# An attention block on one core: x's transposing transfers go one to a body, into waiting places that VectorE copies home, and VectorE writes the projection's bias

## The chip, the cores and the metric

The kernel runs on one core of one Trainium2 chip. The metric is the device time of one execution in microseconds (us). The engines are TensorE (PE; its weight loads are listed as PEld), VectorE (DVE), ScalarE (ACT), GpSimd (POOL) and SyncE (SP), which here issues transfers only. A row with a q behind the engine (SPq, ACTq) belongs to that engine's sequencer.

## What is computed

The reference, cut to what matters (16 batches of 1024 rows of 512 values, 8 heads of 64):

```python
qkv = (x @ w_qkv).reshape(b, n, 3, H, hd).transpose(2, 0, 3, 1, 4)
q, k, v = (qkv[0], qkv[1], qkv[2])
attn = jnp.einsum('bhnd,bhmd->bhnm', q, k) * scale
attn = jnp.where(attn_mask[None, None] == 0, -jnp.inf, attn)
attn = jax.nn.softmax(attn, axis=-1)
o = jnp.einsum('bhnm,bhmd->bhnd', attn, v).transpose(0, 2, 1, 3).reshape(b, n, d)
o = o @ w_proj + b_proj
ln = (o - mu) * jax.lax.rsqrt(var + LN_EPS) * ln_gamma + ln_beta
x = _layernorm(x + (o + ln), axis=-1)
```

## The kernel before

**Bodies.** The work is cut into 64 groups g: one batch (g // 4) and one pair of heads (g % 4). Each engine's program is a row of bodies, one for each group, with one before them and some behind for the last projections. Bodies 5 to 62 are a loop that the engines run from one piece of code; the others stand written out one after another. A body has 8 units (128 query rows each) of 4 slots, and what each engine does in which slot is fixed by tables (`ORDER`, `TAKE_ACT`, `TAKE_DVE`, `NORM_SLOTS`, `XT_UNIT`).

**A head's path.** In a unit, TensorE writes the scores of the two heads of the pair (L401). VectorE adds the mask and takes the row's minimum of the negated scores (L638). ScalarE takes the exponential (L494) and, one unit later, its float16 high part (L507). GpSimd subtracts it for the low part (L742). SyncE then issues one transposing transfer of both parts, `pt<-p_split` (L307, `turn`). `p_split` has 4 places, so that ScalarE's high part of a head waits until the transfer of the head four before it has landed. Three units after the scores TensorE multiplies by V (L422 to L424). There are 16 such transfers in a body. I call a head by its unit and half: (4,b) is the second head of unit 4.

**Side work.** Between these TensorE does the next group's Q and K (`Q0`, `K0`, `K1`, `Q1`; L360), V (`V0`, `V1`; L347), the transposes of the output (`O0`, `O1`; L342) and, four bodies late, the projection of two row tiles (`P0`, `P1`; L383). The first part of the projection's list has 12 matmuls a tile, and a 13th one adds the bias: a matrix of ones times two bias rows (L386). ScalarE and VectorE take each result from one of two PSUM banks as a high and a low part; the next user of the bank waits for that. `O0`, the last transposes of a body, waits for VectorE's low part of K0 (`k_lo`, L627), and that for ScalarE's `k_hi` (L487).

**x.** TensorE needs x transposed (`xt`). Each body loads two tiles of the next batch into `x_in` (L541, ScalarE's queue, slot 1), ScalarE and GpSimd split them into `x_split` (L465, L776), one place for each body of a batch. In the last body of each batch (g % 4 == 3) SyncE issues all four transposing transfers `xt<-x_split` (L285, `turn_x`), two ahead of unit 2's heads and two ahead of unit 3's; in the loop each pair stands under `If((g & 3) == 3)` blocks (L238). `Q0`, which starts in slot 16, waits for the first two, `K1` for the others. The first batch's x goes through the same transfers before the bodies.

**The projection's row tile** is then normalised on VectorE (L667 to L697, in pieces), with the residual and layer norm; `summed` tells that its bank is free.

Of the kernel before, what the change touches and what calls it, by code (L numbers as in the profile page):

```python
# [9 lines left out]
P = 128  # L10
# [18 lines left out]
BIAS_LO = 32  # L29
# [4 lines left out]
ORDER = [("Q1", 0, 12), ("V0", 0, 48), ("V1", 0, 48), ("P0", 0, 4), ("O1", 0, 4), ("P0", 4, 13), ("Q0", 0, 12),  # L34
         ("K0", 0, 12), ("K1", 0, 12), ("P1", 0, 9), ("O0", 0, 4), ("P1", 9, 13)]
# [3 lines left out]
LENGTH = {"Q1": 12, "V0": 48, "V1": 48, "O1": 4, "Q0": 12, "K0": 12, "K1": 12, "O0": 4, "P0": 13, "P1": 13}  # L39
COST = {"Q": 9, "V": 2.5, "O": 5, "K": 9, "P": 9}  # L40
FIRST_GROUP, LAST_GROUP = -1, GROUPS + PAIRS
LOOP = (PAIRS + 1, GROUPS - 1)


def items_by_slot():
# [4 lines left out]
    for kind, i in items:  # L50
# [12 lines left out]
XT_UNIT = [3, 3, 4, 4]  # L63
NORM_SLOTS = [{"stats": 19, "aggr": 20, "eps": 20, "add": 20, "power": 21, "scale": 23, "sum": 24, "stats2": 27,
               "aggr2": 28, "eps2": 28, "power2": 29, "shift": 29, "out": 30},
              {"stats": 30, "aggr": 33, "eps": 33, "add": 34, "power": 35, "scale": 34, "sum": 38, "stats2": 38,
# [72 lines left out]
def attention_block(nc, x, adj, w_qkv, w_proj, b_proj, gamma, beta, out):  # L139
# [3 lines left out]
    with ExitStack() as ctx:  # L143
# [17 lines left out]
        x_split = sb("x_split", [P, T // 2, 2, 2, D], F16)  # L161
        xt = sb("xt", [P, T, 2, KC, P], F16)
# [23 lines left out]
        ones = sb("ones", [P, P], F16)  # L186
        bias_rows = sb("bias_rows", [P, D], F16)
# [8 lines left out]
        x_first = p32[:, :, :].rearrange("p t (two d) -> p t two d", two=2)  # L196
# [12 lines left out]
        bias_ready, bias_zero = sem("bias_ready"), sem("bias_zero")  # L209
        w_hi_ready, w_ready, mask_ready = sem("w_hi_ready"), sem("w_ready"), sem("mask_ready")  # L210
        x_first_loaded, x_in_loaded = sems("x_first_loaded", T // 2), sem("x_in_loaded")
        x_hi_done, x_lo_done, x_turned = sem("x_hi_done"), sem("x_lo_done"), sems("x_turned", 2)
# [22 lines left out]
        def transposing(eng, g, do):  # L235

            if not known(g):
                with eng.If((g & 3) == 3):  # L238
                    do()
            elif (g + 1) % PAIRS == 0 and 0 <= batch(g + 1) < B:  # L240
                do()

# [29 lines left out]
        def _(sp):  # L272
            for t in range(T // 2):
                sp.dma_start(x_first[:, t, :, :], x_pairs[t, :, :, :]).then_inc(x_first_loaded[t], 16)
# [4 lines left out]

            def turn_x(g, p):  # L280

                wait_alone(sp, x_lo_done, batch(g + 1) * (T // 2) + (p + 1))
                if not known(g) or g >= 0:
                    wait_alone(sp, side_ready, side_done(g, "V1"))
                sp.dma_start_transpose(xt[:, 2 * p:2 * p + 2, :, :, :].rearrange("p t h k n -> p (t h k) n"),  # L285
                                       x_split[:, p, :, :, :].rearrange("p t h d -> p (t h d)")
                                       ).then_inc(x_turned[p // 2], 16)

            for p in range(T // 2):
                turn_x(FIRST_GROUP, p)  # L290
# [19 lines left out]

            def body(g):
                for u in range(UNITS):
                    for p in range(T // 2):
                        if u == XT_UNIT[p] and not (known(g) and g == FIRST_GROUP):
                            transposing(sp, g, lambda: turn_x(g, p))
# [10 lines left out]
        def _(pe):  # L326
            pe.wait_ge(ident_ready, 1)

            def side_matmul(g, kind, i):
# [13 lines left out]
                elif kind[0] == "V":  # L343
# [3 lines left out]
                    mm = nc.tensor.matmul(bank[:, c * P:(c + 1) * P], xt[:, t, rows, k, :], w[:, k, OF_V, pair(g), :],  # L347
                                          start=(i == 0), stop=(i % 12 == 11), skip_group_check=True)
                else:
                    k, part = i // 3, i % 3  # L350
                    if part == 0 and known(g) and g < 0 and kind == NEXT_FIRST:
                        pe.wait_ge(w_ready, 2 * (k + 1))
                    if i == 0 and kind == NEXT_FIRST:
                        wait_alone(pe, x_turned[0], batch(g + 1) * 32 + 32)
                    if i == 0 and kind == "K1":
                        wait_alone(pe, x_turned[1], batch(g + 1) * 32 + 32)
                    w, x_half = (w_hi, w_hi, w_lo)[part], (HI, LO, HI)[part]
                    p = pair(g if kind == "Q1" else g + 1)
# [7 lines left out]
            def project(g, half, i):  # L366
                c, t = batch(g - PAIRS), pair(g) * 2 + half
                if i == 0:
                    if known(g) and g == PAIRS and half == 0:
                        pe.wait_ge(w_ready, 4 * KC)  # L370
                        pe.wait_ge(bias_ready, 4)
                    if known(g) and g >= GROUPS:
                        pe.wait_ge(min_done, heads(GROUPS, 0, 0))
                        pe.wait_ge(summed, projected(g, half) - (1 if g > GROUPS or half else 0))
                    else:
                        wait_alone(pe, summed, projected(g, half))
# [4 lines left out]
                if i < 3 * KC:  # L381
                    k, part = i // 3, i % 3
                    mm = nc.tensor.matmul(proj_bank(g, half), ot[:, (HI, LO, HI)[part], parity(c), k, t, :],  # L383
                                          (wp_hi, wp_hi, wp_lo)[part][:, k, :], start=(i == 0), stop=False)
                else:
                    nc.tensor.matmul(proj_bank(g, half), ones[:, :], bias_rows[:, :], start=False, stop=True).then_inc(proj_ready, 1)  # L386
# [39 lines left out]

            def body(g):
# [12 lines left out]
        def _(act):  # L440
# [5 lines left out]
            def prepare_projection():  # L446
                act.wait_ge(wp_loaded, 16 * KC)
                for kc in range(KC):
                    nc.scalar.activation(wp_hi[:, kc, :], wp_in[:, kc, :], ACT.Copy, scale=WSCALE).then_inc(w_hi_ready, 1)
                act.wait_ge(const_loaded, 64)  # L450
                act.wait_ge(bias_zero, 1)
                nc.scalar.activation(bias_rows[0:1, :], x_res[0:1, 0, :], ACT.Copy, scale=WSCALE).then_inc(bias_ready, 1)
                nc.scalar.activation(p_split[BIAS_LO:BIAS_LO + 1, 0, LO, 0:D], x_res[BIAS_LO:BIAS_LO + 1, 0, :], ACT.Copy,
                                     scale=WSCALE).then_inc(bias_ready, 1)

            def first_split(p):
                act.wait_ge(x_first_loaded[p], 16)
                nc.scalar.activation(x_split[:, p, :, HI, :], x_first[:, p, :, :], ACT.Copy).then_inc(x_hi_done, 1)

            def split(g):  # L460
                if known(g) and not 0 <= batch(g) < B - 1:
                    return
                wait_alone(act, x_turned[1], batch(g) * 32 + 32)
                wait_alone(act, x_in_loaded, g * 16 + 16)
# [360 lines left out]
```

## Time and profile before

| | |
|---|---|
| median of 3 runs | 3231.33 us (3230.16 to 3237.03) |
| the profiled execution | 3231.68 us |
| its span in the trace | 3229.8 us |
| PE busy | 2994.3 us (93%) |
| POOL busy | 2628.1 us (81%) |
| ACT busy | 2624.1 us (81%) |
| DVE busy | 2197.0 us (68%) |
| granted TensorE clock | 0.973 |

Busy times are sums over the span. A matmul's end is modelled, so that a busy PE says that it had work, not that it was at its peak. The granted clock is the share of 2.4 GHz that TensorE was given; 0.50 is the lower level, 1.2 GHz.

### The profile page before, as it was taken

What the parts mean: (1) busy time and instruction counts of PE and PEld (TensorE: products, weight loads), DVE (VectorE), ACT (ScalarE), POOL (GpSimd) and SP (SyncE); (2) the same over time, 40 slices, a digit from 0 to 9 for tenths busy, and PEclk for the clock granted to TensorE, in tenths of its full rate; (3) what the DMA queues carried; (4) which work ended last, traced back from release to release, by engine and by line L of the source; (5) the groups of instructions that cost most, each with busy time, mean ns of one, the idle gap of its engine ahead of it and who ended that gap; (6) DMA issues with size and microseconds to landing.
All of it is one profiled execution on the core that took longest, in us unless ns stands there. A gap on an engine that the chain in (4) does not pass through costs nothing.

```text
span 3229.8 us, 119607 instructions
## 1 busy us (share of the span) xinstructions
PE 2994.3 (93%) x42112; PEld 1842.0 (57%) x42112; DVE 2197.0 (68%) x4243; ACT 2624.1 (81%) x3790; POOL 2628.1 (81%) x1610
## 2 busy tenths in 40 slices
PE   5889999899998999999999998999999899999995
PEld 2556556565565556656566565556556566565562
DVE  4546667677676767767677676767767677676775
ACT  5878878788787878878788787888888788787882
POOL 4768878788787878878798797888878788787884
PEclk9989999999999999999999999999999999999997
DMA  8999999999999999999999999999999999999994
GB/s 225 192 199 195 211 214 218 218 208 220 211 212 218 215 214 219 216 212 219 214 216 214 215 213 222 216 215 220 216 214 219 212 212 219 212 215 218 216 208 108
DMA packets 2320778, 682.49 MB, mean 211 GB/s; under 512 B 2268498, under 2 KB 2268498, under 8 KB 2320724
## 3 DMA queue, kind: packets, MB, share of 16 engines
q1 hardware_dynamic: 2266724, 581.58, 97.3%
q10 hardware_dynamic: 54000, 100.16, 9.7%
q8 instruction: 37, 0.61, 0.1%
q14 instruction: 17, 0.14, 0.0%
HBM read 77.60 MB, written 33.55 MB: 34 GB/s over the span
## 4 chain that ended last, share of the span: by engine, by line
POOL 54%; issue 29%; SPq 7%; PE 6%; DMA 2%; DVE 1%; POOLq 1%; ACT 1%; ACTq 0%; DVEq 0%
POOL p_split L742 42%; SPq L307 5%; POOL x_res L758 4%; POOL x_split L776 4%; POOL norm L766 2%; POOL norm L761 2%; PE scores_a L401 1%; PE side L360 1%; SPq L285 1%; DMA pt<-p_split 1%; PE side L347 1%; POOL shift L769 1%; POOLq L741 1%; PE proj L383 0%; PE pv_bank L422 0%
## 5 line engine op out<-in xcount | busy, mean ns | idle before, releaser
L742 POOL TENSOR_TENSOR p_split<-p,p_split 128x1024 f16<-128x1024 f32 x1024 | 2172.4, 2138 | 531.8 <-ACT p_split L507 526.0
L494 ACT ACTIVATE p<-p,row_min 128x1024 f32<-128x1024 f32 x1024 | 1167.9, 1142 | 91.9 <-DVE row_min L638 89.8
L507 ACT ACTIVATE p_split<-p 128x1024 f16<-128x1024 f32 x1024 | 1053.6, 1046 | 206.8 <-DMA pt<-p_split 205.9
L638 DVE CUSTOM_DVE_ANT_0 p<-scores_a,mask_q 128x1024 f32<-128x1024 f32 x512 | 626.9, 1224 | 502.3 <-PE scores_b L401 481.9
L422 PE MATMUL pv_bank<-v_both,pt 128*128 128x64 f16 x8192 | 840.0, 195 | 26.5 <-DMA pt<-p_split 24.6
L424 PE MATMUL pv_bank<-v_both,pt 128*128 128x64 f16 x8192 | 840.6, 195 | 0.0
L423 PE MATMUL pv_bank<-v_both,pt 128*128 128x64 f16 x8192 | 840.5, 195 | 0.0
L422 PEld LDWEIGHTS pv_bank<-v_both,pt 128*128 128x128 f16 x8192 | 747.9, 99 | 115.2 <-issue 39.6
L360 PE MATMUL side<-xt,w_hi 128*128 128x512 f16 x2048 | 683.2, 391 | 119.3 <-DMA xt<-x_split 114.3
L423 PEld LDWEIGHTS pv_bank<-v_both,pt 128*128 128x128 f16 x8192 | 736.9, 99 | 84.4 <-issue 6.0
L424 PEld LDWEIGHTS pv_bank<-v_both,pt 128*128 128x128 f16 x8192 | 737.4, 99 | 0.0
L638 DVE CUSTOM_DVE_ANT_0 p<-scores_b,mask_q 128x1024 f32<-128x1024 f32 x512 | 624.6, 1220 | 6.6 <-POOL p_split L742 0.5
L347 PE MATMUL side<-w_hi,xt 128*128 (+1 forms) x4096 | 399.0, 219 | 1.5 <-DVE q_lo L627 1.5
L360 PE MATMUL side<-xt,w_lo 128*128 128x512 f16 x1024 | 397.9, 389 | 0.0
L360 PEld LDWEIGHTS side<-xt,w_hi 128*128 (+1 forms) x2048 | 187.5, 99 | 349.8 <-issue 221.2
L347 PE MATMUL side<-w_lo,xt 128*128 (+1 forms) x2048 | 367.0, 220 | 0.0
L347 PEld LDWEIGHTS side<-w_hi,xt 128*128 128x128 f16 x4096 | 317.0, 98 | 36.6 <-issue 29.1
L383 PE MATMUL proj<-wp_hi,ot 128*128 128x512 f16 x992 | 329.4, 384 | 2.6 <-issue 2.6
L401 PE MATMUL scores_a<-k_hi,q_hi 64*128 64x512 f16 x1024 | 311.4, 385 | 6.1 <-DVE row_min L638 4.5
L401 PE MATMUL scores_b<-k_hi,q_hi 64*128 64x512 f16 x1024 | 311.6, 385 | 0.0
L401 PE MATMUL scores_b<-k_lo,q_hi 64*128 64x512 f16 x1024 | 304.3, 377 | 0.0
L401 PE MATMUL scores_a<-k_lo,q_hi 64*128 64x512 f16 x1024 | 304.2, 377 | 0.0
(80 smaller groups left out, 4261.3 us busy)
## 6 DMA issues: line engine op xcount, KB each, us to landing
x_in<-in_x ACTq DMA_DIRECT2D x63, 512.0 KB, 5.1
x_res<-in_x ACTq DMA_DIRECT2D x120, 256.0 KB, 3.3
out<-x_res ACTq DMA_DIRECT2D x120, 256.0 KB, 3.7
pt<-p_split SPq DMA_TRANSPOSE x1024, 4.8
pt<-in_adj SPq DMA_DIRECT2D x8, 512.0 KB, 9.7
ot<-in_L_gnn_w_qkv SPq DMA_DIRECT2D x4, 768.0 KB, 9.8
p<-in_x SPq DMA_DIRECT2D x4, 512.0 KB, 5.3
p<-in_x ACTq DMA_DIRECT2D x8, 256.0 KB, 8.5
```

Of the source, the lines that this page charges most:

```text
L307: sp.dma_start_transpose(pt[:, head % TURNED, :, :, :].rearrange("p h t n -> p (h t) n"), p_split[:, head % RING, :, :].rearrange("p h n - ...
L347: mm = nc.tensor.matmul(bank[:, c * P:(c + 1) * P], xt[:, t, rows, k, :], w[:, k, OF_V, pair(g), :], start=(i == 0), stop=(i % 12 == 11), ...
L360: mm = nc.tensor.matmul(bank[:, :].rearrange("p (t n) -> p t n", t=4), w[:, k, what, p, :], xt[:, 4 * half:4 * half + 4, x_half, k, :], st ...
L383: mm = nc.tensor.matmul(proj_bank(g, half), ot[:, (HI, LO, HI)[part], parity(c), k, t, :], (wp_hi, wp_hi, wp_lo)[part][:, k, :], start=(i ...
L401: mm = nc.tensor.matmul(scores[ab][:, keys], left[rows, q], right[rows, keys], start=(n == 0), stop=(n == 2))
L422: nc.tensor.matmul(o, hi, v_hi, start=(kt == 0 and at == 0), stop=False, skip_group_check=True)
L423: nc.tensor.matmul(o, hi, v_lo, start=False, stop=False, skip_group_check=True)
L424: mm = nc.tensor.matmul(o, lo, v_hi, start=False, stop=(kt == T - 1), skip_group_check=True)
L494: nc.scalar.activation(p32[:, slot, :], p32[:, slot, :], ACT.Exp, bias=row_min[:, slot:slot + 1], scale=-1.0, accum_out=row_sum[:, head:he ...
L507: nc.scalar.activation(p_split[:, head % RING, HI, :], p32[:, head % RING, :], ACT.Copy).then_inc(hi_done, 1)
L638: nc.vector.tensor_tensor_reduce(out=p32[:, slot, :], in0=scores[ab][:, :], in1=mask_q[:, u, :], scale=-SCALE, scalar=3.0e38, op0=ALU.add, ...
L742: nc.gpsimd.tensor_tensor(p_split[:, slot, LO, :], p32[:, slot, :], p_split[:, slot, HI, :], ALU.subtract).then_inc(lo_done, 1)
```

## The change

x's transfers: in every body SyncE issues one `turn_x`, ahead of unit 3's heads, without an `If`. It goes to a waiting place at the end of `xt` (the fourth pair of tiles goes straight home). In a batch's last body VectorE copies the six waiting tiles home, one in each of the slots 12 to 17, and `Q0` waits for the last copy (`x_copied`). `K1` of every body waits for that body's transfer. `x_split` has one place instead of four, and x is loaded in slot 12 instead of slot 1. The first batch's x is transposed by TensorE instead, with ScalarE and VectorE splitting it.

The bias: VectorE writes it into the projection's bank (`seed`) after the bank's last reader, and the 12 matmuls add to it; the 13th is gone. The loop ends at body 58 instead of 62, so that bodies 59 to 62 are now written out.

```diff
-ORDER = [... ("P0", 4, 13), ... ("P1", 9, 13)]
+ORDER = [... ("P0", 4, 12), ... ("P1", 9, 12)]
-LOOP = (PAIRS + 1, GROUPS - 1)
+LOOP = (PAIRS + 1, GROUPS - PAIRS - 1)
-XT_UNIT = [3, 3, 4, 4]
+XT_UNIT = 4
+LOAD_X = 12
+COPY = [12, 13, 14, 15, 16, 17]
-               {"stats": 30, "aggr": 33, ...
+               {"stats": 30, "aggr": 31, ...
-        x_split = sb("x_split", [P, T // 2, 2, 2, D], F16)
-        xt = sb("xt", [P, T, 2, KC, P], F16)
+        x_split = sb("x_split", [P, 2, 2, D], F16)
+        xt = sb("xt", [P, T + 6, 2, KC, P], F16)
+        def place(t):
+            return t - 4 if t >= 4 else t + 10
+        def waiting(g):
+            return 8 - pair(g) * 2
+            def turn_x(g):
+                wait_alone(sp, x_lo_done, g + 1)
+                wait_alone(sp, side_ready, side_done(g, "V1"))
+                wait_alone(sp, x_copied, batch(g))
+                sp.dma_start_transpose(xt[:, bass.ds(waiting(g), 2), :, :, :]...
-                    for p in range(T // 2):
-                        if u == XT_UNIT[p] and not (known(g) and g == FIRST_GROUP):
-                            transposing(sp, g, lambda: turn_x(g, p))
+                    if u == XT_UNIT and active(g, "X"):
+                        turn_x(g)
+                    if i == 0 and kind == "K1" and active(g, "X"):
+                        wait_alone(pe, x_turned, g * 16 + 16)
                     if i == 0 and kind == NEXT_FIRST:
-                        wait_alone(pe, x_turned[0], batch(g + 1) * 32 + 32)
-                    if i == 0 and kind == "K1":
-                        wait_alone(pe, x_turned[1], batch(g + 1) * 32 + 32)
+                        wait_alone(pe, x_copied, batch(g + 1))
-                    nc.tensor.matmul(proj_bank(g, half), ones[:, :], bias_rows[:, :], start=False, stop=True).then_inc(proj_ready, 1)
+            def copy_tile(g, t):
+                if t == 0:
+                    wait_alone(dve, side_ready, side_done(g, "V1"))
+                    wait_alone(dve, x_turned, g * 16)
+                move = nc.vector.tensor_copy(xt[:, place(t), :, :, :]..., xt[:, 8 - t // 2 * 2 + t % 2, :, :, :]...)
+            def seed(g, i):
+                nc.vector.tensor_scalar(proj_bank(g, i), bias_b[:, :], WSCALE, None, ALU.mult).then_inc(seeds(g, i)[0], 1)
-                    if s == 1:
+                    if s == LOAD_X:
                         load_next(g)
```

SyncE's program in the loop, around the transfers of units 2 and 3. Before, from the second head of unit 1 to the first head of unit 2 (L307 is a head's transfer, L285 one of x, L238 the `If`, L135 a wait):

```order
L307 DMA_TRANSPOSE pt<-p_split 128x16x128
L238 REGISTER_ALU
L238 COMPARE_AND_BRANCH
L135 ISA x2
L285 DMA_TRANSPOSE xt<-x_split 128x16x128
L238 UNCONDITIONAL_BRANCH
L238 COMPARE_AND_BRANCH
L135 ISA x2
L285 DMA_TRANSPOSE xt<-x_split 128x16x128
L238 UNCONDITIONAL_BRANCH
L135 REGISTER_ALU x2
L307 DMA_TRANSPOSE pt<-p_split 128x16x128
```

The same engine now, from the second head of unit 2 to the first head of unit 3 (L310 is a head's transfer, L319 that of x):

```order
L310 DMA_TRANSPOSE pt<-p_split 128x16x128
L137 REGISTER_ALU
L137 ISA
L137 REGISTER_ALU
L319 REGISTER_ALU x2
L319 ISA
L319 DMA_TRANSPOSE xt<-x_split 128x16x128
L137 REGISTER_ALU x2
L310 DMA_TRANSPOSE pt<-p_split 128x16x128
```

The branches are gone, and the x transfer, which stood under them, now runs in every body between two heads' transfers.

VectorE's program in the loop from the low part of V1 on (slot 12), where unit 3's two masked minima stand. Before:

```order
L621 SCALAR_TENSOR_TENSOR v_both<-side,v_both 128x8x64
L135 REGISTER_ALU
L638 ISA p,row_min<-scores_a,mask_q 128x1024
L638 ISA row_min 128x1
L135 REGISTER_ALU
L638 ISA p,row_min<-scores_b,mask_q 128x1024
```

and now (L655 is a copy, L242 its `If`, L668 the masked minimum):

```order
L641 SCALAR_TENSOR_TENSOR v_both<-side,v_both 128x8x64
L242 REGISTER_ALU
L242 COMPARE_AND_BRANCH
L655 COPY xt<-xt 128x1024
L242 UNCONDITIONAL_BRANCH
L137 REGISTER_ALU
L668 ISA p,row_min<-scores_a,mask_q 128x1024
L668 ISA row_min 128x1
L242 COMPARE_AND_BRANCH
L655 COPY xt<-xt 128x1024
```

A copy under an `If` now stands between each two of VectorE's steps here; the sixth one stands behind unit 4's first masked minimum.

## Rows read from the trace of the kernel before

**Rows 1.** The page, its first line.

```profile
span 3229.8 us, 119607 instructions
```

**Rows 2.** Windows: a body with one batch's heads only, and a batch's last body.

```profile
core 0: us, PE busy (x) PEld busy (x) DVE busy (x) ACT busy (x) POOL busy (x), PEclk, DMA share, GB/s
1120.90:1167.20 46.30, 45.79 (x659) 28.33 (x658) 34.05 (x66) 40.86 (x60) 40.87 (x26) 1.00 1.08 214
1167.20:1222.90 55.70, 48.07 (x661) 29.29 (x661) 34.05 (x66) 40.75 (x60) 40.99 (x26) 0.94 1.10 217
```

**Rows 3.** Waits: waiter, releaser, us in total, times, longest us.

```profile
ACT p_split L507 <- DMA pt<-p_split: 205.9, 216, 3.3
...
PE side L360 <- DMA xt<-x_split: 114.3, 16, 26.1
```

**Rows 4.** Timeline of SP: issues of head (7,a), three bodies (start us, us).

```profile
1125.56 3.07 SPq L307 DMA_TRANSPOSE pt<-p_split  x1
...
1171.84 3.56 SPq L307 DMA_TRANSPOSE pt<-p_split  x1
...
1227.49 3.42 SPq L307 DMA_TRANSPOSE pt<-p_split  x1
```

**Rows 5.** Timeline of ACT: high part of head (6,b), the same two bodies.

```profile
1162.59 1.06 ACT L507 ACTIVATE p_split<-p 128x1024 f16<-128x1024 f32 x1 [1.13 <-DMA pt<-p_split]
...
1218.25 1.06 ACT L507 ACTIVATE p_split<-p 128x1024 f16<-128x1024 f32 x1 [1.16 <-DMA pt<-p_split]
```

**Rows 6.** Timeline of SP: issues around the two places with `If` blocks.

```profile
1140.52 2.38 SPq L307 DMA_TRANSPOSE pt<-p_split  x1
...
1143.62 1.95 SPq L307 DMA_TRANSPOSE pt<-p_split  x1
...
1145.86 3.77 SPq L307 DMA_TRANSPOSE pt<-p_split  x1
...
1150.30 1.92 SPq L307 DMA_TRANSPOSE pt<-p_split  x1
```

**Rows 7.** Line L307, single transfers issued at 1119.5, 1121.9 and 1125.6.

```profile
DMA to landing us min/median/max: 4.5/4.5/4.5
...
DMA to landing us min/median/max: 6.1/6.1/6.1
...
DMA to landing us min/median/max: 6.2/6.2/6.2
```

**Rows 8.** Groups by line: shapes xcount | busy us, mean ns | idle before.

```profile
L742 POOL TENSOR_TENSOR p_split<-p,p_split 128x1024 f16<-128x1024 f32 x1024 | 2172.4, 2138 | 531.8 <-ACT p_split L507 526.0
...
L386 PE MATMUL proj<-bias_rows,ones 128*128 128x512 f16 x124 | 48.8, 393 | 0.0
...
L594 DVE TENSOR_SCALAR mask_q<-pt 128x1024 bf16<-128x1024 f32 x8 | 5.3, 686 | 11.8 <-DMA pt<-in_adj 11.8
```

**Rows 9.** Timelines of DVE and PE around Q0 in a batch's last body.

```profile
1191.72 1.23 DVE L638 CUSTOM_DVE_ANT_0 p<-scores_a,mask_q 128x1024 f32<-128x1024 f32 x1 [1.19 <-PE scores_b L401]
...
1197.43 0.61 PE L360 MATMUL side<-xt,w_hi 128*128 128x512 f16 x1 [5.69 <-DMA xt<-x_split]
```

**Rows 10.** Windows: the stretch of low clock behind that wait.

```profile
1195.00:1201.80 6.80, 4.37 (x32) 2.45 (x33) 0.00 (x0) 0.62 (x2) 1.69 (x1) 0.50 1.06 196
```

**Rows 11.** Windows: batches 2 and 14, the first and last of 13; body 4; bodies 60 to 62.

```profile
442.60:637.30 194.70, 185.90 (x2635) 114.56 (x2636) 136.63 (x265) 164.13 (x238) 164.45 (x101) 0.98 1.09 217
...
2778.60:2972.90 194.30, 185.80 (x2635) 114.37 (x2636) 135.40 (x263) 162.25 (x235) 163.19 (x100) 0.98 1.08 214
2972.90:3111.00 138.10, 137.24 (x1975) 84.91 (x1974) 101.95 (x198) 121.87 (x178) 122.34 (x76) 1.00 1.09 217
...
239.60:287.80 48.20, 47.11 (x661) 28.52 (x658) 30.28 (x58) 39.93 (x59) 39.24 (x22) 0.97 1.16 195
```

**Rows 12.** Timeline at the start: PE waits for the low part of Q0.

```profile
38.87 1.01 PE L360 MATMUL side<-xt,w_hi 128*128 128x512 f16 x2 [5.02 <-DVE q_lo L627]
```

**Rows 13.** Timeline of DVE in the last projections.

```profile
3203.53 0.75 DVE L686 SCALAR_TENSOR_TENSOR p<-scores_a,norm,p 128x512 f32<-128x512 f32 x1 [1.51 <-POOL norm L761]
```

More of the change, by code:

```diff
@@ L233, in bodies, with at_end @@
                 body(g)
[L235 removed]
+        def at_end(eng, g, do):
             if not known(g):
@@ L257, in proj_bank, with seeds @@
             return scores[0][:, 0:CH] if known(g) and g >= GROUPS and i == 1 else proj[:, :]
+        def seeds(g, i):
+            if known(g) and g >= GROUPS:
+                return (seeded[0], projected(GROUPS, 0) + (g - GROUPS + 1)) if i == 0 else (seeded[1], g - GROUPS + 1)
+            return seeded[0], projected(g, i) + 1
         def last_tile(g, i):
@@ L327, in _, with first_turn @@
             pe.wait_ge(ident_ready, 1)
+            def first_turn(t):
+                pe.wait_ge(x_first_loaded[t], 16)
+                wait(pe, x_first_lo, t - 1)
+                for k in range(KC):
+                    mm = nc.tensor.transpose(side[t % 2][:, k * P:(k + 1) * P], x_first[:, t, k * P:(k + 1) * P], ident[:, :])
+                mm.then_inc(x_first_turned, 1)
             def side_matmul(g, kind, i):
@@ L370, in project @@
                         pe.wait_ge(w_ready, 4 * KC)
[L371 to L376, printed above, removed]
+                    wait_alone(pe, *seeds(g, half))
                     if half == 0:
@@ L425, in times_v @@
                 mm.then_inc(pv_done, 1)
+            for t in range(T):
+                first_turn(t)
+            for k in range(KC):
+                mm = nc.tensor.matmul(proj[:, k * P:(k + 1) * P], ident[:, :], ident[:, :], start=(k == 0), stop=True,
+                                      skip_group_check=True)
+            mm.then_inc(bits_set, 1)
             def body(g):
@@ L449, in prepare_projection, with first_high @@
                     nc.scalar.activation(wp_hi[:, kc, :], wp_in[:, kc, :], ACT.Copy, scale=WSCALE).then_inc(w_hi_ready, 1)
[L450 to L464, printed above, removed]
-                nc.scalar.activation(x_split[:, pair(g), :, HI, :], x_in[:, :, :], ACT.Copy).then_inc(x_hi_done, 1)
+            def first_high(t):
+                act.wait_ge(x_first_turned, t + 1)
+                nc.scalar.activation(xt[:, place(t), HI, :, :], side[t % 2][:, :].rearrange("p (k n) -> p k n", k=KC), ACT.Copy
+                                     ).then_inc(x_first_hi, 1)
             def take(g, kind):
```

150 lines of the change are left out of this document (81 added, 69 removed).

## The prediction

> **What bounds the kernel now.** I read the body's length first. A body takes 46.3 us, and a batch's last body 55.7 [rows 2]; 13 batches in a row take 2530.3 us, 194.6 each [rows 11]. So a batch's last body costs 9.4 us more than the others, and the obvious reason is the wait that the change goes for: TensorE waits 114.3 us in 16 pieces for x's transfers [rows 3], 5.7 us of it in the body shown [rows 9], and behind it the clock is at its lower level (0.50, 1.2 GHz) for 6.8 us [rows 10], which loses 3.4. Together 9.1 of the 9.4 us. In the other bodies TensorE has work for 45.8 of 46.3 us [rows 2], which looks like a kernel that TensorE bounds.
>
> Then I followed the other engines round a body, because ScalarE also waits for transfers, 205.9 us in 216 pieces [rows 3]. SyncE's queue issues head (7,a) at 1125.56, 1171.84 and 1227.49 [rows 4]: laps of 46.28 and 55.65 us, the bodies' own lengths. Each lap has two legs. On the first, SyncE issues twelve heads with next to nothing between them, until (4,b) lands; that lets ScalarE write the high part of (6,b), which the trace shows as a wait ended by a transfer, at 1162.59 and at 1218.25 [rows 5]. On the second leg come ScalarE's steps up to the high part of (7,a), GpSimd's low part and the next issue of (7,a). The second leg is 9.25 us in the one body and 9.24 in the other. The first is 37.03 and 46.41 us. **So the lap is made of the transfer leg and a fixed rest, in both kinds of body,** and the last body's 9.38 us are four x transfers in the queue's leg. TensorE's wait is a second road to nearly the same length, and taking it away alone gives nothing back. This is the step on which all else rests.
>
> **An x transfer in every body.** It is issued between (2,b) and (3,a), within the first leg. Four of them lengthen it by 9.38 us [rows 4, 5], 2.35 each. But the body without x transfers pays for the `If` blocks: SyncE stands still for 0.72 us (1142.90 to 1143.62) and 0.67 us (1149.63 to 1150.30), where 0.29 is usual (1145.57 to 1145.86) [rows 6], 0.8 us too much, and the change drops them. If such gaps cost their full length, an x transfer is (9.38 + 0.8) / 4 = 2.55 us and the change adds 2.55 - 0.8 = 1.75 a body; if they cost nothing it adds 2.35. I take 1.7, since the queue has no idle time in this leg into which a gap could fall.
>
> **The load of x_in** moves from slot 1 to slot 12. Now it lies across the start of the leg: a head's transfer takes 4.5 us to land before it, and 6.1 (outside the leg) and 6.2 us (its first) beside it [rows 7]. In slot 12 all it delays is inside. If the second delay is only the first one handed on, moving costs nothing; if they are two, 1.6 us. I take 0.5, nearer the lower end, as 6.2 also holds a store of the same time.
>
> A body is then 46.3 + 1.7 + 0.5 = **48.5 us**, with bounds 46.3 + 1.7 = 48.0 and 46.3 + 2.35 + 1.6 = 50.3. Below that I keep 47.4 as a rival.
>
> **What TensorE saves.** Two bias matmuls a body, at most 0.39 us each [rows 8], so TensorE needs about 45.4 of the 48.5 us. This is worth nothing: it makes TensorE's wait at `O0` longer, which is where a late lap shows. `K1` waits in each body for its own x transfer; that lands about when K1 starts, and a wait there comes out of the 3 us at `O0`.
>
> **VectorE's seeds** are two more steps a body of at most 0.69 us (L594, twice their elements [rows 8]), beside 34 us of work in 46 [rows 2]: hidden in the bodies. In the last projections VectorE idles only 1.51 us at a time for GpSimd [rows 13], once in two tiles, so of 1.4 us a pair of tiles some 0.9 shows, four times: +3.5.
>
> **The copies** are six in a batch's last body. The trace has no copy between float16 tiles; the nearest row is L594, 1024 elements from SBUF to SBUF in 0.69 us [rows 8], and I take that, between 0.3 and the 1.23 us of the masked minimum [rows 9]. The sixth copy stands behind unit 4's first masked minimum, which starts at 1191.72, about when TensorE is ready for Q0 (1197.43 - 5.69 = 1191.74) [rows 9]. So Q0 cannot start before 1191.7 + 1.2 + 0.7 + 0.2 for the semaphore: TensorE waits 2.1 us, and 2.6 if copies two to five make VectorE half a microsecond late. If the clock then halves for half as long as in rows 10, this costs another 1.7. TensorE's road through the last body is 45.4 + 0.3 + 2.6 + 1.7 = 50.0, longer than the lap; with 0.3 for what is left of an earlier low clock, 50.3 us.
>
> **The sum.** A batch: 3 x 48.5 + 50.3 = 195.8 against 194.6, +1.2, and 13 of them +15.6. Batches 0 and 1 hold eight x transfers before and after: +1. Bodies 60 to 62 take 46.0 us each; they leave the loop, and straight-line body 4, which has no x transfer either, takes 48.2 [rows 11]: +6.5. At the start TensorE waits 5.0 us for Q0's low part [rows 12], which stands behind mask tiles whose loads SyncE issues after the x transfers; without these some 3 us go. Last projections +3.5. Together 15.6 + 1 + 6.5 - 3 + 3.5 = +23.6: a span of 3253.4 [rows 1], and with the 1.9 us outside it (3231.68 - 3229.8) 3255.3. The profiled execution is 0.35 us above the median of the runs. **Forecast: 3255 us**, with 3234 to 3285 as its own range (48.1 to 49.1 a body).
>
> **The rivals.**
>
> *The transfer leg grows less (chance 0.20).* If the gaps cost more than their length, or the moved load falls into time that the dropped `If` opens, a body is 47.4 and the last 49.3: 191.5 a batch, -40 in 13, and +5 outside: 3196 us. For it: the laps scatter, and the leg of 37.03 us holds other loads and stores. Against: nothing in rows 4 and 5 shows a transfer cheaper than 2.35.
>
> *TensorE is the bound after all (0.08).* Then a body is 45.7, the last 48.1 (2.4 of wait), 185.2 a batch, -122 in 13 and +1 outside: 3111 us. For it: 45.8 of 46.3 us busy. Against: the second leg's 9.24 and 9.25 us.
>
> *The copies stand still for GpSimd (0.22).* This is one mechanism on the other side of no change, and it decides from about 1 us per copy on. GpSimd's low part runs 2.14 us [rows 8], one after another. If a copy cannot run beside it, each of the last four or five waits for the rest of one; by hand the sixth ends at about 1199, so that TensorE waits 7.5 us, more than now, with a longer low clock: 45.4 + 0.3 + 7.5 + 2.8 = 56.0 for the last body, 5.7 more than above in 15 batches, +85: 3340 us. The trace cannot speak for or against it: VectorE's wide steps there read PSUM, and L594 ran while GpSimd had no work. The Trainium skill speaks for it: "SBUF — State Buffer", section "Who interferes with whom", says that VectorE and GpSimd share a port pair under an exclusive lock, held for a whole instruction, when VectorE runs in a two-port mode; and "VectorE: DVE Perf Modes", section "The perf-mode tier table", puts a 16-bit copy within SBUF into such a mode, at four elements a cycle. By the second page alone a copy would take an estimated 0.4 us (1024 elements at four a cycle and the fixed cost that it gives) and the last body would be some 0.3 us shorter; by both pages, the 3340 stands. No run shows either yet.
>
> *The low clock comes in every body (0.06).* A wait of about 3 us at `O0` may halve the clock each time; it decides once TensorE's road passes the lap, 48.5 - 45.4 = 3.1 us, that is if 3 us of wait and more than 0.1 of lost clock add up. With 50 us a body and 51.8 the last: 201.8 a batch, 3333 us.
>
> *The time is only moved (0.06).* The four transfers cost the same wherever they stand, and all else cancels: 3232 us.
>
> **From these to the numbers.** The forecast has 0.38. A measurement of this kernel can tell about 0.2%, 6.5 us, from no change. Faster by more: 0.19 of the first rival, the second's 0.08: 0.27. Within it: 0.06, 0.01 of the first and 0.04 of the forecast's lower edge: 0.11. Slower: the rest of the forecast 0.34, 0.22 and 0.06: 0.62. The range 3185 to 3335 leaves out the second rival, about half of the third and some of the fourth, under 2 in 10.
>
> **What would show it.** SyncE's laps: 48 to 49 us between issues of (7,a) in every body, the second leg still 9.2 us, TensorE's wait at `O0` grown from under 1 us to 2 or 3. A copy's duration, and when the sixth ends against the masked minimum before it: right behind it, and the last body is about 50 us; 5 us later, and it is the lock. The prediction is wrong if the second leg shrinks when the first grows, for then the lap was not what it seemed; or if bodies come down to 45.6.

## The result and the profile after

The changed kernel takes 3360.73 us (median of 4 runs, 3353.94 to 3365.36), the kernel before in runs beside it 3232.34: the ratio is 1.0394, with a 95% interval of 1.0371 to 1.0416. It is slower, as forecast, but by 128 us instead of 24, and it lies 26 us above the range.

The page's first line, to [rows 1]:

```profile
span 3363.5 us, 119057 instructions
```

The span grew by 133.7 us. I cut it at the bodies' starts as before [rows 11]. Windows of a batch's four bodies (24 to 27), of the two stretches of low clock in them, of bodies 8 to 11 (batch 2), of bodies 60 to 62 and of all behind them; columns as in [rows 2]:

```profile
1259.70:1308.40 48.70, 45.76 (x657) 27.93 (x656) 35.22 (x68) 40.97 (x60) 41.51 (x27) 1.00 1.04 210
1308.40:1358.00 49.60, 46.40 (x657) 28.07 (x656) 35.61 (x69) 41.66 (x61) 41.64 (x26) 0.98 1.07 214
1358.00:1407.80 49.80, 46.63 (x657) 28.14 (x656) 34.81 (x68) 40.23 (x59) 40.41 (x26) 0.98 1.05 208
1407.80:1461.30 53.50, 47.12 (x657) 29.02 (x656) 42.45 (x74) 41.39 (x60) 41.09 (x25) 0.94 1.00 201
1356.40:1359.80 3.40, 3.40 (x24) 1.17 (x22) 1.96 (x5) 3.29 (x6) 1.83 (x2) 0.51 1.15 212
1434.90:1441.80 6.90, 3.39 (x30) 2.02 (x31) 4.89 (x7) 2.48 (x4) 2.85 (x2) 0.51 0.97 189
447.70:650.00 202.30, 186.19 (x2595) 112.30 (x2595) 146.74 (x276) 163.07 (x234) 162.88 (x101) 0.97 1.03 205
3085.90:3232.00 146.10, 138.36 (x1971) 84.66 (x1972) 105.63 (x205) 118.73 (x176) 117.36 (x74) 0.99 1.14 196
3232.00:3363.50 131.50, 78.72 (x865) 44.97 (x864) 76.94 (x160) 49.59 (x70) 65.85 (x62) 0.79 0.69 125
```

A plain body is 48.7 to 49.8 us, where I had 48.5, and the last one 53.5, where I had 50.3. The 13 batches of [rows 11] went from 194.6 to 202.9 us each: 108 of the 133.7 us. The rest lies in the bodies behind them (257.0 us before, 277.6 now) and before them (5.1).

SyncE's issues of (7,a), to [rows 4] (timeline of SP, four laps):

```profile
1264.74 2.29 SPq L310 DMA_TRANSPOSE pt<-p_split  x1
...
1313.42 2.42 SPq L310 DMA_TRANSPOSE pt<-p_split  x1
...
1362.29 1.89 SPq L310 DMA_TRANSPOSE pt<-p_split  x1
...
1412.82 2.32 SPq L310 DMA_TRANSPOSE pt<-p_split  x1
...
1466.32 2.31 SPq L310 DMA_TRANSPOSE pt<-p_split  x1
```

Laps of 48.7, 48.9, 50.5 and 53.5 us. TensorE's side of it, to [rows 3] (waits: waiter, releaser, us in total, times, longest):

```profile
ACT p_split L519 <- DMA pt<-p_split: 318.3, 251, 3.2
...
PE side L359 <- DVE k_lo L647: 129.6, 49, 3.8
...
PE side L380 <- DVE xt L655: 79.8, 15, 5.5
...
PE side L380 <- DMA xt<-x_split: 22.8, 37, 2.1
```

The wait for x's transfers (114.3 us) became one for the copies at `Q0`, 5.3 us in the mean of the last bodies (5.5 in the loop), and one of 2.6 us at `O0` in every plain body. In bodies 8 to 57 low clock follows the first in all 12 last bodies, the second in 18 of 38 plain ones. Now VectorE and GpSimd in that last body (timelines; L655 is a copy, L668 the masked minimum, L786 GpSimd's low part, L802 its bias):

```profile
1426.42 0.42 DVE L655 COPY xt<-xt 128x1024 f16<-128x1024 f16 x1
1426.75 1.22 DVE L668 CUSTOM_DVE_ANT_0 p<-scores_a,mask_q 128x1024 f32<-128x1024 f32 x1
...
1427.89 1.93 DVE L655 COPY xt<-xt 128x1024 f16<-128x1024 f16 x1
...
1431.49 4.28 DVE L655 COPY xt<-xt 128x1024 f16<-128x1024 f16 x3
1435.69 1.21 DVE L668 CUSTOM_DVE_ANT_0 p<-scores_a,mask_q 128x1024 f32<-128x1024 f32 x1
...
1436.83 1.20 DVE L655 COPY xt<-xt 128x1024 f16<-128x1024 f16 x1
```

```profile
1427.41 4.41 POOL L786 TENSOR_TENSOR p_split<-p,p_split 128x1024 f16<-128x1024 f32 x2
1431.77 1.45 POOL L802 TENSOR_TENSOR x_res<-x_res,beta_b 128x512 f32<-128x512 f32 x1
1433.27 4.49 POOL L786 TENSOR_TENSOR p_split<-p,p_split 128x1024 f16<-128x1024 f32 x2
```

What it does to the transfers (timeline of SP, heads (3,a), (3,b) and (4,a); the masked minimum of (4,a) is the one at 1435.69, behind three copies):

```profile
1439.48 4.94 SPq L310 DMA_TRANSPOSE pt<-p_split  x2
...
1448.26 1.91 SPq L310 DMA_TRANSPOSE pt<-p_split  x1
```

SyncE is done with the first two at 1444.42 and issues the third at 1448.26: 3.8 us idle inside the transfer leg, where 0.3 is usual there in a plain body. A smaller gap stands in every body, ahead of x's own transfer (L319), from 1436.67 to 1437.41, 0.7 us, where 0.3 is usual:

```profile
1424.54 12.13 SPq L310 DMA_TRANSPOSE pt<-p_split  x4
1437.41 1.78 SPq L319 DMA_TRANSPOSE xt<-x_split  x1
```

Line L655, all 90 copies (duration in ns: min/median/max):

```profile
L655 DVE COPY xt<-xt x90: 414/1204/2343, 209.3 to 3061.7; 128x1024 f16<-128x1024 f16 x90
```

One and the same copy takes 0.41 us, as the first one does, beside a GpSimd step of 128x1 only, or anything up to 2.34. The second begins at 1427.89, inside GpSimd's pair of low parts that began at 1427.41, and ends at 1429.82; the first of the two low parts ends at 1429.54, 0.3 us before it. GpSimd pays too: two low parts take 4.49 us where [rows 8] gives 2 x 2.14, and the bias 1.45 us.

### The profile page after: what moved, and what is told of

It reads as the page before. It is cut to its first block, busy times and chain, and to the rows that moved or that the text cites. A ratio compares the mean times of both kernels' runs of the same rounds, so it can differ in the third digit from the quotient of the medians.

```text
span 3363.5 us, 119057 instructions
## 1 busy us (share of the span) xinstructions
PE 3016.6 (90%) x42024; PEld 1833.9 (55%) x42024; DVE 2382.6 (71%) x4466; ACT 2635.4 (78%) x3789; POOL 2626.5 (78%) x1603
## 4 chain that ended last, share of the span: by engine, by line
POOL 34%; issue 22%; PE 20%; SPq 12%; DMA 5%; DVE 4%; ACT 1%; POOLq 1%; DVEq 0%; ACTq 0%
POOL p_split L786 27%; SPq L310 11%; PE scores_a L416 5%; DMA pt<-p_split 4%; PE side L364 4%; PE side L380 4%; POOL x_res L802 3%; POOL x_split L820 2%; PE proj L397 2%; PE pv_bank L437 2%; PE pv_bank L439 2%; PE pv_bank L438 2%; POOL norm L810 1%; SPq L319 1%; DVE xt L655 1%
## 5 line engine op out<-in xcount | busy, mean ns | idle before, releaser
L786 POOL TENSOR_TENSOR p_split<-p,p_split 128x1024 f16<-128x1024 f32 x1024 | 2180.2, 2144 | 661.4 <-ACT p_split L519 654.3
L668 DVE CUSTOM_DVE_ANT_0 p<-scores_a,mask_q 128x1024 f32<-128x1024 f32 x512 | 626.3, 1223 | 413.5 <-PE scores_b L416 323.6
L668 DVE CUSTOM_DVE_ANT_0 p<-scores_b,mask_q 128x1024 f32<-128x1024 f32 x512 | 623.9, 1219 | 3.4 <-POOL p_split L786 0.6
L397 PE MATMUL proj<-wp_hi,ot 128*128 128x512 f16 x992 | 315.8, 391 | 4.4 <-DVE proj L625 4.4
L416 PE MATMUL scores_b<-k_lo,q_hi 64*128 64x512 f16 x1024 | 311.1, 385 | 0.0
L416 PE MATMUL scores_a<-k_lo,q_hi 64*128 64x512 f16 x1024 | 311.1, 385 | 0.0
```

Of the source, the lines that this page charges most:

```text
L416: mm = nc.tensor.matmul(scores[ab][:, keys], left[rows, q], right[rows, keys], start=(n == 0), stop=(n == 2))
L668: nc.vector.tensor_tensor_reduce(out=p32[:, slot, :], in0=scores[ab][:, :], in1=mask_q[:, u, :], scale=-SCALE, scalar=3.0e38, op0=ALU.add, ...
L786: nc.gpsimd.tensor_tensor(p_split[:, slot, LO, :], p32[:, slot, :], p_split[:, slot, HI, :], ALU.subtract).then_inc(lo_done, 1)
```

## The experiments

All start from the changed kernel. Times stand against the kernel before, run beside each of them. The table gives mean body lengths in bodies 8 to 57 by place in the batch, worked out from the times at which unit 0's scores start in each trace, and the mean of 13 batches (bodies 8 to 59). e1, e4 and e11 leave something out and e12 adds a part of the projection twice: they price a term and are no kernels to use. The code is cut to the lines that matter.

| kernel | 1st | 2nd | 3rd | last | batch | median | ratio to before (95%) |
|---|---|---|---|---|---|---|---|
| before | 46.2 | 46.2 | 46.2 | 56.0 | 194.6 | 3232.3 | |
| after | 49.3 | 49.9 | 49.8 | 54.0 | 202.9 | 3360.7 | 1.0394 (1.0371 to 1.0416) |
| e1 small copies | 49.7 | 49.6 | 49.5 | 51.1 | 199.8 | 3313.1 | 1.0244 (1.0222 to 1.0266) |
| e2 reduce copies | 49.2 | 49.5 | 49.6 | 53.6 | 201.9 | 3349.4 | 1.0357 (1.0328 to 1.0386) |
| e3 load early | 48.6 | 48.7 | 49.2 | 53.9 | 200.3 | 3324.5 | 1.0280 (1.0259 to 1.0301) |
| e4 no seed | 49.2 | 49.9 | 49.7 | 54.1 | 203.0 | 3360.1 | 1.0386 (1.0353 to 1.0418) |
| e5 between bodies | 46.2 | 48.5 | 49.5 | 55.8 | 199.8 | 3318.8 | 1.0266 (1.0249 to 1.0283) |
| e6 pair copies | 50.0 | 49.5 | 49.6 | 49.8 | 198.9 | 3299.1 | 1.0200 (1.0180 to 1.0220) |
| e7 all three | 45.7 | 48.0 | 48.1 | 51.6 | 193.7 | 3231.2 | 0.9996 (0.9987 to 1.0006) |
| e8 idle Ifs | 49.5 | 50.1 | 50.3 | 54.8 | 204.8 | 3381.4 | 1.0459 (1.0441 to 1.0476) |
| e9 copies later | 45.6 | 48.1 | 48.0 | 50.2 | 192.3 | 3211.7 | 0.9935 (0.9916 to 0.9954) |
| e10 load in 20 | 47.3 | 49.5 | 48.7 | 51.2 | 196.6 | 3271.5 | 1.0120 (1.0100 to 1.0140) |
| e11 tiny x | 47.7 | 47.8 | 46.7 | 54.0 | 196.2 | 3271.5 | 1.0122 (1.0100 to 1.0145) |
| e12 more matmuls | 49.2 | 49.0 | 48.7 | 54.6 | 201.6 | 3343.5 | 1.0340 (1.0320 to 1.0359) |

**e1, the copies' time.**

```diff
-move = nc.vector.tensor_copy(xt[:, place(t), :, :, :]..., xt[:, 8 - t // 2 * 2 + t % 2, :, :, :]...)
+move = nc.vector.tensor_copy(xt[:, place(t), 0, 0, 0:2], xt[:, 8 - t // 2 * 2 + t % 2, 0, 0, 0:2])
```

> The six copies of a batch's last body move 2 elements instead of 1024 (x's tiles don't come home, so that Q, K and V of later batches are made of old x). Theory A (the copies, stretched by GpSimd's low parts, hold up the heads behind them, and the transfer queue runs dry in unit 4): a batch's last body falls from about 53.9 us to that of the others, 49.7, the second leg from 10.7 to 9.45, TensorE's wait at Q0 from 5.5 to under 0.5 us: 15 x 4.1 = 62 us less, 3300 us. Theory B (the copies' time lies beside the transfer leg and only TensorE's wait at Q0 moves elsewhere): under 10 us less, above 3350.

48 us less, nearer to A. The last body falls to 51.1 us, not to 49.7, and TensorE still waits 2.9 us at `Q0` (waits of e1). But this run does not take the copies' time away: line L655 and the second copy of a batch with GpSimd's pair of low parts beside it (timelines of e1):

```profile
PE side L380 <- DVE xt L655: 42.9, 15, 2.9
...
L655 DVE COPY xt<-xt x90: 156/441/2021, 205.1 to 3015.5; 128x2 f16<-128x2 f16 x90
...
1212.25 1.94 DVE L655 COPY xt<-xt 128x2 f16<-128x2 f16 x1
...
1212.03 4.23 POOL L785 TENSOR_TENSOR p_split<-p,p_split 128x1024 f16<-128x1024 f32 x2 [0.15 <-ACT p_split L519]
```

A copy of 2 elements takes 0.16 us or up to 2.02. The one shown begins inside a low part and ends with it (at 1214.19; half of the pair's 4.23 us is over at 1214.15), and the six of a batch still take 5.2 us of VectorE's time, against 8.0. So most of a copy's time is standing still and has nothing to do with its length. The shorter copies, which no longer stretch GpSimd's steps either, are worth 2.4 us of the wait and 2.9 us of the body; what the place of the sixth copy alone costs, behind unit 4's first masked minimum, this run doesn't show.

**e2, another form of the same copy.**

```diff
-move = nc.vector.tensor_copy(out, in_)
+move = nc.vector.tensor_reduce(out, in_.rearrange("... (n o) -> ... n o", o=1), axis=X, op=ALU.max)
```

> The copy is written as a tensor_reduce over an axis of one element, which moves the same 1024 elements. Theory A (the copy alone takes GpSimd's port and stands still for its step; this form does not): all six take one and the same time, about 1.1 us by the masked minimum's 1.22, whether GpSimd works beside them or not, GpSimd's steps beside them stay at 2.14 us instead of 2.3; the six sum to 6.7 us instead of 8.0 and the sixth ends 1.3 us earlier: 15 x 1.3 = 20 us less, 3341 us. Theory B (the stretching comes from GpSimd's own reads of SBUF and meets every form of VectorE's step): steps of up to 1.1 + 2.1 = 3.2 us, the sum above 9 us, 3375 us or more.

Line L655 and GpSimd's steps around 1432 in the trace of e2:

```profile
L655 DVE TENSOR_REDUCE xt<-xt x90: 1207/1211/1219, 209.4 to 3050.2; 128x1024 f16<-128x1024 f16 x90
```

```profile
1430.34 1.28 POOL L803 TENSOR_TENSOR x_res<-x_res,beta_b 128x512 f32<-128x512 f32 x1
1432.09 4.21 POOL L787 TENSOR_TENSOR p_split<-p,p_split 128x1024 f16<-128x1024 f32 x2 [0.46 <-ACT p_split L519]
```

All 90 take 1.21 us, beside GpSimd's steps or not, and these keep their 2.14 and 1.28 us. Same data, same places, same neighbours: the stretching belongs to the form of the copy. The median is 11 us lower though a lone copy takes three times as long; the intervals of the two ratios overlap, so that gain is at the edge of the noise, and it is the durations that rule out B. The six sum to 7.3 us here, against 8.0. What six copies of 0.42 us would cost unhindered, no run shows.

**e3, the load of x_in back in slot 1.**

```diff
-LOAD_X = 12
+LOAD_X = 1
-    wait_alone(act, x_lo_done, g + 1)
-    act.dma_start(x_in[:, :, :], x_pairs[g + (PAIRS + 1), :, :, :])
+    wait_alone(act, x_lo_done, g)
+    act.dma_start(x_in[:, :, :], x_pairs[g + PAIRS, :, :, :])
```

> x_in's load back in slot 1 (of the body that splits it), all else as after. Theory A (my term: in slot 12 the load lies inside the transfer leg and costs 0.5 us a body or more): 60 x 0.5 = 30 us less, 3331 us; the leg from the issue of (7,a) to the landing of (4,b) falls from 39.2 to about 38.7 us. Theory B (its place does not matter, as it delays one head's transfer wherever it stands): within 7 us of 3361. Theory C (the load is what makes x's transfer late for K1 and the clock fall at O0, so that it costs about 1.3 us in two bodies of four more): 3290 us.

36 us less, 0.6 a body, where I had 0.5: A. In the plain bodies it is 0.7, 1.1 and 0.6 us, 0.8 on average, and next to nothing in the last one, where SyncE's gap ahead of (4,a) grows from 4.2 us on average to 5.6 and takes it up. Low clock follows the wait at `O0` about as often as before (17 of 38 plain bodies), so that C is not what happens. `K1`'s wait for its x transfer falls from 22.8 to 4.7 us with it.

**e4, the seeds.**

```diff
-nc.vector.tensor_scalar(proj_bank(g, i), bias_b[:, :], WSCALE, None, ALU.mult)
+nc.vector.tensor_scalar(proj_bank(g, i)[:, 0:2], bias_b[:, 0:2], WSCALE, None, ALU.mult)
-    start=False
+    start=(i == 0)
```

> VectorE writes 2 of the bias's 512 columns (the bias is left out of the others) and TensorE's first matmul overwrites the bank: the seed keeps its place and its signals, its time falls from 0.70 to about 0.15 us. Theory A (hidden behind the laps in the bodies, seen only in the last projections): 3 us less, 3358 us. Theory B (VectorE's added work in units 1 and 6 delays the masked minimum behind it, and through ScalarE and GpSimd the transfer queue): 0.3 us or more a body, 3340 us or less.

No difference in the medians (0.6 us): the seeds are hidden.

**e5, x's transfers between the bodies.** `turn_x` no longer waits for V1 there, since the waiting place is free.

```diff
-if u == XT_UNIT and active(g, "X"): turn_x(g)
+if u == 0: with sp.If((g & 3) != 0): turn_x(g - 1)
-if u == XT_UNIT: turn_x(g)
+if u == XT_UNIT: with sp.If((g & 3) == 3): turn_x(g, True)
-wait_alone(pe, x_turned, g * 16 + 16)
+wait_alone(pe, x_turned, batch(g + 1) * 64)
```

> The x transfers of a batch's first three pairs go one body later, ahead of the issue of (7,a), where SyncE stands idle 1.1 to 2.5 us in the trace of after; only the fourth pair's stays in unit 4 of the last body. Theory A (a body's length is the transfer leg from the issue of (7,a) to the landing of (4,b), and x's transfer costs what it adds to that leg): the leg of the first three bodies falls by 2.0 to 2.4 us, from 39.6 to about 37.4, the second leg grows by 0.5 to 1.0 us, so a plain body is 1.5 us shorter and the last body no longer than now: 13 x 4.5 = 60 us less, 3300 us. Theory B (the DMA queues are the bound wherever the transfer stands in the lap): the body keeps its length, within 7 us of 3361.

42 us less, two thirds of A. By the definition of [rows 4, 5] the first leg of the three bodies fell from 40.1 to 36.8 us, by more than A has it, but the second grew from 9.5 to 11.9, not by 0.5 to 1.0. The timeline of SP shows why (L320 is the x transfer):

```profile
1346.07 2.15 SPq L320 DMA_TRANSPOSE xt<-x_split  x1
1348.55 3.34 SPq L310 DMA_TRANSPOSE pt<-p_split  x1
```

It is issued with (7,a) right behind it, so that it fills little of the idle time and pushes (7,a) back. The second leg is fixed only as long as nothing is put into it. The edit also brings two `If` blocks into each body of the loop, in e7, e9 and e10 too; e8 prices four of them at some 0.4 us a body.

**e6, three copies of two tiles, two of them behind V0.**

```diff
-COPY = [12, 13, 14, 15, 16, 17]
+COPY = [10, 11, 15]
+if t != 1: wait_alone(dve, side_ready, side_done(g, "V0" if t == 0 else "V1"))
+move = nc.vector.tensor_copy(xt[:, (10, 12, 0)[t]:(12, 14, 2)[t], :, :, :]..., xt[:, 8 - 2 * t:10 - 2 * t, :, :, :]...)
+if t == 1: move.then_inc(x_near, 1)      # Q0 waits for this one, K1 for x_copied
```

> Three copies of two tiles instead of six of one, in slots 10, 11 (behind V0 alone, for the tiles that Q0 and K0 read) and 15 (for K1), so that GpSimd's step can hold VectorE up three times at most and none of it stands between V1 and Q0. Theory A (copies and their place cost the last body 4.1 us): the wait at Q0 is gone, the clock does not fall there, the last body is 49.8 to 50.8 us: 15 x 3.5 = 53 us less, 3308 us. Theory B (the held-up VectorE delays the heads of units 2 and 3 just as much as before): the wait at Q0 goes, the last body stays above 52.5 us, 3340 us or more.

62 us less: A, and 9 more. The last body is 49.8 us, like the others; the wait at `Q0` and the gap ahead of (4,a) are gone. This is the run that shows that the copies, as they stood, made the last body 4 us longer. The copies are still held up (line L657; twice the elements):

```profile
L657 DVE COPY xt<-xt x45: 679/1470/1912, 205.4 to 3001.3; 128x2048 f16<-128x2048 f16 x45
```

**e7, e5 + e6 + e3.**

> The edits of e5_between_bodies, e6_pair_copies and e3_load_early together. If the three costs are separate and add up: 3361 - 60 - 53 - 36 = 3212 us, 0.6% below before, with bodies of 47.0 us and a last one of 49.5. If TensorE's road (46.0 us a body with its waits for low parts) or the second leg becomes the bound, bodies stay at 47.5 us or more and the time is 3235 us or more.

129 us less, against 140 for the sum of the three: they add up but for 11 us. It is level with the kernel before. In its last body, 51.6 us, TensorE waits 3.8 us (once 4.2) for V's low part, which stands behind the copies of slots 10 and 11 on VectorE (waits of e7, in which 0.7 us each in other bodies are counted too):

```profile
PE pv_bank L448 <- DVE v_both L652: 78.4, 43, 4.2
```

**e8, the price of the `If` blocks.**

```diff
+if u in (3, 4) and not known(g):
+    for _ in range(2):
+        with sp.If((g & 3) == 3): sp.nop()
```

> Two If blocks with a no-op under them ahead of the heads of unit 2 and two ahead of those of unit 3, as the kernel before had them. Theory A, as the prediction had it (SyncE has no idle time in the transfer leg, so that the 0.8 us for which the branches hold it up lengthen the body in full): 54 x 0.8 = 43 us more, 3404 us. Theory B (two transfers are under way when the gap comes, and the landing of the next is not late): the gap shows on SyncE, the leg keeps its length, 3361 us within 7.

21 us more, 0.38 a body: half of my 0.8, between the theories. It is an upper price of the gaps themselves: plain bodies grow by 0.3 us, the last one by 0.8, and low clock stands behind `O0` in 25 of 38 plain bodies instead of 18.

**e9, the copies of e7 in slots 12, 13 and 17.**

```diff
-COPY = [10, 11, 15]
+COPY = [12, 13, 17]
```

> e7_all_three with its copies in slots 12, 13 and 17 instead of 10, 11 and 15, so that they stand behind VectorE's low parts of V0 and V1 (the trace of e7 shows TensorE waiting 3.8 us in a batch's last body for v_both's low part). Theory A (that wait is what makes its last body 51.5 us against 48.1): the wait falls below 1 us and the last body to 49.5 us, 15 x 2 = 30 us less than e7's 3231: 3201 us. Theory B (the copies cost the same wherever they stand, as the wait only moves to Q0 or K1): within 7 us of 3231.

20 us less than e7: A, though short of 30 (the last body is 50.2 us). One batch of e9 in windows:

```profile
1204.00:1249.30 45.30, 45.23 (x657) 28.06 (x656) 35.12 (x68) 40.66 (x60) 40.62 (x25) 1.00 1.09 220
1249.30:1297.10 47.80, 45.60 (x657) 28.03 (x656) 35.17 (x68) 40.55 (x60) 41.44 (x27) 1.00 1.09 219
1297.10:1345.00 47.90, 45.57 (x657) 28.04 (x656) 35.15 (x68) 40.53 (x60) 41.02 (x26) 1.00 1.09 219
1345.00:1394.60 49.60, 45.71 (x657) 28.19 (x656) 40.47 (x71) 40.86 (x60) 41.82 (x25) 1.00 1.10 222
```

The clock doesn't fall in this batch, nor in any plain body of 8 to 57; in last bodies it falls in 5 of 12. V's low part is no longer waited for longer than 0.7 us in the loop, but in each last body TensorE now waits 2.5 us ahead of unit 4's scores for a masked minimum, since VectorE is late with its steps (waits of e9):

```profile
PE scores_a L427 <- DVE row_min L682: 42.6, 27, 2.8
```

This is the version that beats both kernels, the one before by 0.65%.

**e10, e9 with the load in slot 20.**

```diff
-LOAD_X = 1
+LOAD_X = 20
```

> e9_copies_later with the load of x_in in slot 20 (for the next body) instead of slot 1. Theory A (the DMA queues are busy all through the lap, and the load delays the transfers beside it alike wherever it stands): within 7 us of e9. Theory B (in slot 1 it meets the x transfer between two bodies, and both fall into the leg up to (7,a)): 0.5 us a body or more shorter, 3175 us or less.

60 us more than e9, 1.0 a body: both theories fall. The load does not cost the same everywhere. In slot 20 it lies in the first leg (37.4 us in the three plain bodies, 35.3 in e9), and the second gets only 1.2 us shorter for its absence. It is e3's result again, with a higher price; part of that is low clock, which follows a wait in 10 of 38 plain bodies here and in none of e9.

**e11, x's transfer taken away.**

```diff
-sp.dma_start_transpose(xt[:, bass.ds(waiting(g), 2), :, :, :]..., x_split[:, :, :, :]...)
+sp.dma_start(xt[:, bass.ds(waiting(g), 2), 0, 0, 0:2], x_split[:, :, 0, 0:2])
```

> After with x's transfer of bodies 5 to 59 replaced by a plain transfer of 2 by 2 elements with the same signals (x's later tiles are left out: old ones are used), to price the transfer in the leg by itself. With the price of 2.35 us that the four of the kernel before show, and hardly anything for the small one: 55 x 2.3 = 127 us less, 3234 us, the leg in plain bodies 37.3 us. With my net 1.7 us: 3267 us. If the added transfer is not what made the bodies longer (the clock and the load are): less than 1 us a body, above 3305.

89 us less. Plain bodies lose 1.6, 2.1 and 3.1 us, 2.3 on average, the price of [rows 4, 5], of which some 0.3 is low clock that no longer comes (9 of 38 plain bodies instead of 18); the first leg loses 2.2. The last body loses nothing (54.0): SyncE's gap ahead of (4,a) grows from 4.2 to 5.6 us instead, as the copies hold the head up anyway. That the time lands near the 3267 of the net price is luck; it is the full price in three bodies of four.

**e12, TensorE kept busy at `O0`.**

```diff
+if kind == "O0" and i == 0 and active(g, "P1"):
+    for again in range(3, 9): project(g, 1, again)
```

> After with six matmuls of P1 (items 3 to 8) done a second time ahead of O0, where TensorE waits 2.6 us in each body (part of the projection is added twice). Theory A (the wait lets the clock fall in some plain bodies, 1.7 and 2.0 us of low clock a body in the second and third of a batch, and these bodies are 0.7 us longer for it): TensorE has 2.3 us more work in time in which it waited, the low clock behind O0 is gone, 10 to 20 us less, 3345 us. Theory B (the leg alone sets these bodies): within 7 us of 3361. Theory C (the added work is late for the scores behind it): 3375 us or more.

17 us less for 2.3 us more of matmuls a body: A. The three plain bodies of a batch in windows:

```profile
1255.90:1305.00 49.10, 46.98 (x663) 28.55 (x662) 35.21 (x68) 40.94 (x60) 40.43 (x26) 1.00 1.02 205
1305.00:1354.30 49.30, 47.02 (x663) 28.51 (x662) 35.21 (x68) 40.95 (x60) 40.98 (x26) 1.00 1.06 213
1354.30:1403.10 48.80, 47.06 (x665) 28.55 (x666) 35.21 (x68) 41.03 (x60) 41.10 (x26) 1.00 1.06 215
```

The granted clock is 1.00 throughout, where it was 0.98 in two of the three, and no plain body of 8 to 57 has low clock. By the table's means the sum of the three bodies falls by 2.1 us; the last body, in which TensorE has no such wait at `O0`, is 0.6 longer.

## Why the prediction was wrong

**The bound was read rightly.** The kernel before was held by its lap, not by TensorE: TensorE's wait for x's transfers went from the last body, and every plain body became longer. With x's transfer gone (e11), plain bodies came back by its price.

**The copy was mis-sized; this is the step that failed most.** I priced it by L594 at 0.69 us and let `Q0` wait 2.6 us. A lone copy takes 0.41 us, one beside GpSimd's wide steps up to 2.34, and the six add up to 8.0 us. My rival of the copies that stand still (0.22) is what happened in kind: in e1 a copy of 2 elements stands still as well, e2 shows that it is the form of the copy, and GpSimd's steps show that they are held up in turn. It was too dear as I worked it out, a wait of 7.5 us and a last body of 56.0; measured were 5.3 to 5.5 and 54.0. TensorE's road held as a sum: with the measured wait (5.5) and what the low clock takes from a last body (3.6, where I had 2.0) it is 45.4 + 5.5 + 3.6 = 54.5. But I had looked at that road alone, and the same copies let SyncE's queue run dry, for some 4 us ahead of (4,a) in each last body, so that the lap came to 54.2 us by itself (legs of 44.0 and 10.2). Which of the two roads ends last, no run separates; e6 removes both. Against my 50.3 this is 3.7 us a batch. By the Trainium skill, "SBUF — State Buffer", section "Who interferes with whom", a copy in a two-port mode and GpSimd exclude each other for a whole instruction: the trace agrees (0.41 against 2.34 us). The same section of the Trainium skill says that `tensor_reduce` never contends on this chip: e2 agrees (1207 to 1219 ns). The Trainium skill's "VectorE: DVE Perf Modes", section "The perf-mode tier table", gave an estimated 0.4 us for the lone copy: 414 ns measured.

**The `If` gaps were half as dear.** "The queue has no idle time in this leg into which a gap could fall" was false: e8 charges 0.38 us at most for 0.8 us of gaps. With that an x transfer is (9.38 + 0.38) / 4 = 2.44 us and the change adds 2.44 - 0.38 = 2.06 a body, 0.36 more than I took: 1.1 a batch. I also gave the new transfer no gap of its own; SyncE stands still 0.4 us longer than usual ahead of it (0.7 against 0.3), and no run prices that.

**The clock in plain bodies was left out of the likeliest case.** I saw the wait at `O0` grow to "2 or 3 us" (it is 2.6) and gave the low clock behind it 0.06 as a rival for every body. It comes behind 18 of 38, and e12 puts it at 2.1 us a batch.

**The load** was nearly right: 0.6 a body measured by e3 (0.8 in plain bodies), 0.5 taken. **The seeds** in the bodies were right (e4).

Together 3.7 + 1.1 + 2.1 = 6.9 of the 7.1 us by which a batch is longer than my 195.8, and the load's further 0.3 in three bodies would make it 7.8: the terms overlap, and the sum is no closer than that; 13 batches make 92 of the 110 us by which the span passes my 3253.4. The other 18 lie at the ends. I had -3 + 1 up to body 8 and +6.5 + 3.5 behind body 59; measured are +5.1 and +20.6. Bodies 60 to 62 went from 138.1 to 146.1 us, 8.0 for my 6.5. For the rest, from 118.8 to 131.5 behind body 63, no run was made; the traces of the twelve experiments, one of each, give 123.4 (e4) to 130.3 us there (e5), so that the cause of this part stays open.

**"The second leg is fixed"** held in plain bodies as long as nothing was put into it (9.5 us on average in before and after, where I had read 9.25 off one body; 10.2 in the last body after) and failed in e5 and e7 (11.9 and 13.1), where the first leg gave back more than the second took. Only their sum, the lap, is a length that one can count on.

## What to carry to other kernels

Before a copy is priced by a row of the same engine, ask what runs beside it. Here GpSimd was busy 78% of the time, and a 16-bit copy within SBUF cost what was left of GpSimd's step each time, even one of 2 elements; fewer and larger copies, placed early behind the last reader, were worth 62 us, more than the copy's form. When an ablation makes a step short, look at its duration in the trace before reading its price off the time: e1's copies were short in elements only. In a queue that is nearly always busy a transfer cost its full price in the first leg (2.3 us, e11), and moving it between the bodies gave back part of that (42 us in all, e5), because what it no longer took from one leg it put into the other. And when a change adds a wait of some 2.6 us to each round of a TensorE loop, as here, put the low clock that may follow it into the sum, not only among the rivals.

## What the runs showed that I had not expected

- Six extra matmuls (2.3 us) in a wait of 2.6 us made the kernel 17 us faster, while the granted clock stayed at 1.00 (2.4 GHz) in the plain bodies.
- A copy of 2 elements took up to 2.02 us beside GpSimd's low parts, against 0.16 alone (e1).
- The blocking goes both ways: 44 of GpSimd's 1024 low parts took over 2.2 us in the changed kernel, none in the kernel before, in e2 or in e6, where 45 larger copies were stretched as well.
- Moving one load of 512 KB was worth 0.6 us a body in e3 (from slot 12 of one body to slot 1 of the next), and 1.0 us between e9 and e10 (slot 1 against slot 20 of the body before).
